# Causal attention as one stream of 32 units, x loaded at its start, and a shared buffer for the last store of each stage

## The reference

```python
# layer 0 attention, per batch b; positions rotate pairs of q and k (RoPE)
q[h] = rope(x @ Wq[h].T)          # 2 heads of 128
k    = rope(x @ Wk.T)             # one key head, shared
v    = x @ Wv.T                   # one value head, shared
p[h] = softmax(q[h] @ k.T / sqrt(128) + causal mask)
out  = concat_h(p[h] @ v) @ Wo.T
y    = layernorm(x + out)
```

## Time and profile before

| what | value |
|---|---|
| median of 3 runs | 2108.05 us (2103.53 to 2110.74) |
| the profiled execution's own time | 2110.27 us |
| its span, first to last instruction | 2108.4 us |
| PE busy | 1884.2 us, 89% of the span |
| DVE, ACT, POOL busy | 75%, 59%, 28% |
| attention | from 0 to about 279.4 us of the span |
| later stages begin at | 283.7, 565.3, 902.8, 1511.6 and 1967.9 us |
| mean granted clock of TensorE | 0.94 of full speed |

### The profile page before, as it was taken

How to read it: one execution, slowest core, us unless ns; L and a number is a source line. 1 busy time by engine, 2 the same in 40 slices (tenths; PEclk the granted TensorE clock), 3 DMA queues, 4 the chain that set the end, 5 groups by cost and what they waited for, 6 DMA issues and landing times. The chain is left out here.

```text
span 2108.4 us, 32001 instructions
## 1 busy us (share of the span) xinstructions
PE 1884.2 (89%) x10615; PEld 1281.7 (61%) x10624; DVE 1571.8 (75%) x3786; ACT 1249.2 (59%) x2554; POOL 597.4 (28%) x767
## 2 busy tenths in 40 slices
PE   7999979999599999669999999999799998995697
PEld 5667644444377777548888887888673444544342
DVE  4554547677447888659999999999533999997498
ACT  3335436656345555168888887887313768876465
POOL 2221216678302222200000000000000777777022
PEclk9999989999699999689999999999768999998799
DMA  2000020000200000000000000000310222222100
GB/s 91 30 30 0 30 88 11 15 6 11 89 22 11 21 11 11 6 20 2 6 16 1 6 16 6 2 7 16 132 62 2 53 59 63 63 68 67 48 26 26
DMA packets 34697, 65.80 MB, mean 31 GB/s; under 512 B 8406, under 2 KB 19743, under 8 KB 33783
## 3 DMA queue, kind: packets, MB, share of 16 engines
q1 hardware_dynamic: 26358, 47.16, 6.6%
q0 software_dynamic: 8192, 16.79, 3.1%
HBM read 51.34 MB, written 12.58 MB: 30 GB/s over the span
## 5 line engine op out<-in xcount | busy, mean ns | idle before, releaser
L2183 DVE SCALAR_TENSOR_TENSOR pk_level<-pk_sums,pk_least 128x1024 f32<-128x1024 f32 x256 | 322.3, 1279 | 22.8 <-ACT pk_sums L2092 21.6
L2092 ACT ACTIVATE pk_sums<-pk_sum 128x512 f32<-128x512 f32 x512 | 278.7, 602 | 94.5 <-PE pk_sum L2302 92.2
L2524 POOL DMA_INDIRECT tk_values<-top_keys_values,tk_index x256 | 241.8, 945 | 197.1 <-DVE tk_index L2744 119.4
L2310 PE MATMUL pk_weights<-product_keys_early_ident,pk_level 128*128 128x128 f32 x2048 | 269.5, 274 | 26.3 <-DVE pk_level L2183 24.3
L2310 PEld LDWEIGHTS pk_weights<-product_keys_early_ident,pk_level 128*128 128x128 f32 x2048 | 226.0, 141 | 52.9 <-DVE pk_level L2183 33.8
L2954 PE MATMUL tk_to_act<-tk_keys,tk_xT 128*128 128x512 f32 x512 | 236.0, 611 | 22.5 <-ACT tk_scores L2611 21.2
L2954 PEld LDWEIGHTS tk_to_act<-tk_keys,tk_xT 128*128 128x128 f32 x512 | 96.2, 195 | 144.2 <-issue 94.7
L1755 PEld LDWEIGHTS er_outs<-experts_early_w,er_hT 128*128 128x128 f32 x1024 | 134.0, 192 | 59.8 <-issue 56.4
L1165 PE MATMUL ml_outs<-experts_early_we,ml_xT 128*128 128x512 f32 x320 | 160.1, 628 | 3.5 <-DVE ml_r L1022 3.5
L2302 PE MATMUL pk_sum<-pk_lay_corners,pk_partsT 96*128 96x256 bf16 x1024 | 154.1, 272 | 0.9 <-ACT pk_sums L2092 0.9
L2742 DVE MAX8 tk_best<-tk_scores 128x8 f32<-128x4096 f32 x32 | 141.2, 4413 | 14.9 <-ACT tk_scores L2611 14.9
(11 more groups left out here) (437 smaller groups left out, 3700.0 us busy)
## 6 DMA issues: line engine op xcount, KB each, us to landing
tk_scores<-top_keys_compress SPq DMA_DIRECT2D x1, 4096.0 KB
tk_values<-top_keys_values,tk_index POOLq DMA_INDIRECT x256, 2.5
att_x_proj<-x_first SPq DMA_DIRECT2D x4, 512.0 KB, 5.3
att_x_res<-x_first SPq DMA_DIRECT2D x4, 512.0 KB, 4.3
x_after_attention<-att_y SPq DMA_DIRECT2D x4, 512.0 KB, 5.0
experts_early_w<-experts_w SPq DMA_DIRECT2D x2, 1024.0 KB
x_after_attention<-ml_y SPq DMA_DIRECT2D x8, 256.0 KB, 2.0
experts_ahead_x<-x_after_attention SPq DMA_DIRECT2D x8, 256.0 KB, 3.4
```

The source lines that it names most:

```text
L2092: act.activation(sums[:, n % SUMS, half * HALF:(half + 1) * HALF], bank[:], ACT.Copy).then_inc(S.free.sem, 1)
L2183: dve.scalar_tensor_tensor(level[:, n % LEVELS, :], sums[:, n % SUMS, :], least[:, t % 2, h:h + 1], sums[:, n % SUMS, :], ALU.is_ge, ALU.m ...
L2310: ins = pe.matmul(weights[:, ch * P:(ch + 1) * P], level[:, n % LEVELS, ch * P:(ch + 1) * P], ident[:], is_transpose=True, start=h == 0 an ...
L2524: pool.indirect_dma_start(out=values[:, slot, k, :], out_offset=None, in_=c["values"], in_offset=bass.IndirectOffsetOnAxis(ap=index[slot][ ...
```

## The change

**Attention becomes one stream.** The loop is gone. 32 units (4 batches of 8) run one behind the other, and the work of a head (now called preparing) is cut in pieces, which PE, ACT, DVE and POOL do between the units of the batch before. The first batch's pieces run before the first unit. In preparing:

- q and k of one tile are a single matmul: xT of the tile stays in the array, 384 columns of weights pass (8 for each batch; swapped weights are no longer needed).
- DVE multiplies the 384 columns with cos, and twice 192 of them, read with a step of 2, with sin. POOL adds 384 columns. PE then transposes three blocks (q of two heads, k) through ring A, and ACT copies them out in two instructions, of 256 and 128 columns.
- Wv and Wo are multiplied with each other once, at the start. v becomes 256 columns wide, so the values' matmul gives the output itself: the copy by DVE and the matmul with Wo are gone. For each block of keys the transposed probabilities of a head stay in the array and 128 columns of v pass: two matmuls of 128 columns instead of one of 256.
- All four batches of x are loaded at the beginning, behind the constants, and kept in SBUF.

**The last store of each stage** but the final one leaves from a buffer (`last`) that belongs to both the stage and the next one. The stage does not wait for its landing; SP waits for it in the next stage (`first_x.stored`), ahead of its loads.

```diff
 class Ahead:
         self.x, self.arrived = room.sb("x", shape), room.sem("arrived")
+        self.last, self.stored = room.sb("last", [P, PER_HALF, P]), room.sem("stored")
...
+        PROJECTED = {1: (0, 1), 2: (2, 3), 3: (4,), 4: (5,), 5: (6,), 6: (7,)}
+        TURNED = {2: (0, 1), 3: (2,), 4: (3, 4), 5: (5,), 6: (6,), 7: (7,)}
+        VALUED = {1: (0,), 2: (1,), 3: (2,), 4: (3,)}
...
+        def in_turn(u):
+            return ([("xT", g) for g in range(HALVES)] if u == 0 else []) + [("qk", t) for t in PROJECTED.get(u, ())] + \
+                   [("v", g) for g in VALUED.get(u, ())] + [("qkT", t) for t in TURNED.get(u, ())]
...
 # SP
+            sp.dma_start(x[:, 0], x_in[0]).then_inc(x_loaded[0], 16)
...
+            for b in range(1, B):
+                sp.dma_start(x[:, b], x_in[b]).then_inc(x_loaded[b], 16)
             next_weights.load(sp)
...
+            sp.wait_ge(y_ready, B * HALVES)
+            sp.dma_start(x_out[B - 1][:, PER_HALF:TILES, :], next_x.last[:]).then_inc(next_x.stored, 16)
+            for i in range(2):
+                sp.wait_ge(stored[i], 16 * (B // 2))
...
 # DVE
+            def turn(b, t):
...
+                dve.tensor_tensor(turned[:, q % 2, 0], both, spread(cos[:, t, :], 1, HEADS + 1), ALU.mult)
+                dve.tensor_tensor(turned[:, q % 2, 1, :, 0::2], both[:, :, 1::2], spread(sin[:, t, 0::2], 1, HEADS + 1), ALU.mult)
+                dve.tensor_tensor(turned[:, q % 2, 1, :, 1::2], both[:, :, 0::2], spread(sin[:, t, 1::2], 1, HEADS + 1),
+                                  ALU.mult).then_inc(V.free.sem, 1)
...
+            for n in range(-UNITS, ALL + 2):
+                if 0 <= n + 1 < ALL:
+                    maxes(n + 1)
+                if 1 <= n <= ALL:
+                    residual(n - 1)
+                if n < ALL and prepared(n):
+                    b, u = prepared(n)
+                    for t in PROJECTED.get(u, ()):
+                        turn(b, t)
+                if n >= 2:
+                    normalise(n - 2)
...
 # PE
+            def project(b, t):
+                pe.wait_ge(A.free.sem, taken_from_A("xT", b, t // PER_HALF))
+                bank = claim_V()
+                pe.matmul(bank[:, 0:COLS], xT[:, t * P:(t + 1) * P], wqk[:], start=True, stop=True).then_inc(V.full.sem, 1)
...
+                        ins = pe.matmul(bank[:, own], probsT[:, n % 2, k, own], v[:, b % 2, k, own],
+                                        start=k == 0 and h == 0, stop=k == u and h == HEADS - 1)
...
+            multiply_weights()
+            for n in range(-UNITS, ALL + 1):
+                if 0 <= n + 1 < ALL:
...
+                    score(n + 1)
+                if n >= 1:
+                    weigh_values(n - 1)
+                if 0 <= n < ALL:
+                    transpose_probs(n)
+                if n < ALL and prepared(n):
...                                   (the pieces of in_turn(u) for the next batch)
...
 # SP of the next stage (here the second one; the third and fourth likewise)
+            sp.wait_ge(first_x.stored, 16)
             load(1)
...
-            sp.wait_ge(stored[1], 16 * B)
+            sp.wait_ge(stored[1], 16 * (B - 1))
```

More of the change, by code:

```diff
@@ new lines, in take_wvo, with take_xT @@
+            def take_wvo():
+                act.wait_ge(wvo_full, 1)
+                act.activation(wvo[:], scores[:, 0, 0:HEADS * P], ACT.Copy).then_inc(wvo_ready, 1)
+            def take_xT(b, g):
+                act.wait_ge(A.full.sem, A.to_take(0))
+                bank = A.take()
+                if b > 0:
+                    act.wait_ge(V.full.sem, made_for_V("qk", b - 1, TILES - 1))
+                act.activation(xT[:, g * HALF:(g + 1) * HALF], bank[:], ACT.Copy).then_inc(A.free.sem, 1)
@@ new lines, in take_probsT @@
+            def take_probsT(n, j):
+                blocks = min(2, n % UNITS + 1 - 2 * j)
+                act.wait_ge(A.full.sem, A.to_take(0))
+                bank = A.take()
+                if j == 0 and n >= 2:
+                    act.wait_ge(V.full.sem, made_for_V("out", n - 2))
+                act.activation(probsT[:, n % 2, 2 * j:2 * j + blocks, :].rearrange("p k n -> p (k n)"),
+                               bank[:, 0:blocks * HEADS * P], ACT.Copy).then_inc(A.free.sem, 1)
+            take_wvo()
@@ new lines, in maxes, with residual @@
+            def maxes(n):
+                keys = (n % UNITS + 1) * P
+                for h in range(HEADS):
+                    dve.wait_ge(scored, n * HEADS + h + 1)
+                    after(dve, exped, (n - KEPT + 1) * HEADS)
+                    dve.tensor_reduce(neg_max[:, n % KEPT, h:h + 1], scores[:, h, 0:keys], AX.X, ALU.max,
+                                      negate=True).then_inc(maxed, 1)
+            def residual(n):
+                b, u = divmod(n, UNITS)
+                s = n % KEPT
+                dve.wait_ge(exped, (n + 1) * HEADS)
+                steps.link(dve.reciprocal(inv_sum[:, s, :], row_sum[:, s, :]))
+                dve.wait_ge(V.full.sem, V.to_take(0))
+                bank = V.take()
+                if u == 0:
+                    dve.wait_ge(x_loaded[b], 16)
+                steps.link(dve.scalar_tensor_tensor(r1[:, n % 2, :], bank[:, 0:P], inv_sum[:, s, 0:1],
+                                                    x[:, b, u, :], ALU.mult, ALU.add))
+                dve.scalar_tensor_tensor(r[:, s, :], bank[:, P:2 * P], inv_sum[:, s, 1:2], r1[:, n % 2, :],
+                                         ALU.mult, ALU.add).then_inc(V.free.sem, 1)
+                dve.wait_ge(V.free.sem, taken_from_V("out", n))
+                norm_stats(steps, dve, r[:, s:s + 1, :], stats[:, s:s + 1, :],
+                           moments[:, s:s + 1, :]).then_inc(moments_ready, 1)
@@ new lines, in normalise @@
+            def normalise(n):
+                b, u = divmod(n, UNITS)
+                s = n % KEPT
+                dve.wait_ge(rstd_ready, n + 1)
+                if u == 0:
+                    after(dve, stored[b % 2], 16 * (b // 2))
+                own = y[:, b % 2, u:u + 1, :]
+                if b == B - 1 and u >= PER_HALF:
+                    own = next_x.last[:, u - PER_HALF:u - PER_HALF + 1, :]
+                last = norm_apply(dve, own, r[:, s:s + 1, :], moments[:, s:s + 1, :], rstd[:, s:s + 1])
+                if u % PER_HALF < PER_HALF - 1:
+                    steps.do(last)
+                else:
+                    steps.settle()
+                    last.then_inc(y_ready, 1)
@@ L2203, in normalise @@
                 after(dve, stored[g % 2], 16 * (g // 2))
[L2204 removed]
+                own = next_x.last if g == GROUPS - 1 else y[:, g % 2]
+                norm_apply(dve, own, r[:], moments[:], rstd[:]).then_inc(y_ready, 1)
             norm_x(0)
```

492 lines of the change are left out of this document (237 added, 255 removed).

## The result

The changed kernel takes **2073.05 us** in the median (4 runs, 2071.28 to 2074.04); the kernel before, on the same chip, 2109.36 (4 runs, 2103.53 to 2110.74). The ratio is 0.9829, 95% interval 0.9813 to 0.9845: 1.7% less time, well clear of the noise, though under 2%. Forecast were 2067 us and a range of 2054 to 2084. One execution of a later kernel, first_batch, took 3148.54 us at a mean granted clock of 0.55 and stands in no median here. The profiled execution took 2072.89 us, with a span of 2070.7 and a mean granted clock of 0.94, as before.

A forecast was written before the change was run, and what follows sets the result against it. The prediction took PE's work and waits to bound attention. From 2110.3 us profiled it took off 32.7 for attention and 8.2 for stage ends, giving 2069.4, or 2067 against the median 2.2 lower; range 2054 to 2084.

The forecast's parts named there:

- What bounds the batch: Attention's stream: PE's order sets the batch, 53.2 us of work plus 4.8 of waits, 58.0 a batch.
- The sum unit by unit: PE's waits in attention, added over small and large units: 3.7 us a batch.
- unseen hand-overs: PE's waits in attention: hand-overs not visible cost more than nothing, so 4.8 us a batch was taken over 3.7.
- The rival with bare loads: Attention's values: 72 more weight loads cost 0.11 each, 7.9 us a batch, 32 in all, total 2099; chance 0.03.
- DVE, ACT, POOL: Attention: their work hides behind PE in the units, DVE at some 34 us and ACT 33 of 58.
- The beginning: Attention's start: DVE's 1.2 us a tile sets the pace, first scores at about 23.8 instead of 26.2, unit 1's at 25.2.
- The sum for attention: All of attention: PE ends at 243.9, last y at 246.7 instead of 279.4, a gain of 32.7 us.
- Stage ends: Five stage ends: barriers come earlier by SP's wait, 2.3, 1.9, 1.7, 0.3 and 2.0, sum 8.2 us, bounds 4 and 10.1.
- The rival by which stage ends give nothing: Stage ends: the next stage starts on something else, or the barrier takes what was won; 2075 us; chance 0.07.
- I count nothing: Pause at attention's end: PE still falls to half clock there, so no gain or loss was taken for the clock.
- The series exchange: Attention: PE waits for each step between engines, 76 us a batch, total 2141, slower than before; chance 0.03.
- The stream that fills nothing: Attention: PE waits as long as before, 8.4 us a batch, total 2079, with head costs 2083; chance 0.13.

The follow-up runs named there:

- first_batch: Changed kernel with only batch 0's pieces reordered, so what unit 0 doesn't need goes behind it; median 2061.41 us, ratio to before 0.9774.
- more_pe: Changed kernel plus two matmuls of 128 columns in each unit, results unused; 2191.79 us, ratio to before 0.9864, on a slower chip.
- ring_order: Changed kernel with only the order of pieces changed, moving transposes of q and k apart from v's fill; 2182.85 us, ratio to before 0.9792, slower chip.
- await_all: Changed kernel with the wait for the last store put back at all five stage ends; 2200.43 us, ratio to before 0.9886, slower chip.
- await_first: Changed kernel with the wait for the last store put back at attention's end only; 2196.12 us, ratio to before 0.9835, slower chip.
- both_orders: Changed kernel with the piece orders of ring_order (batches 1 to 3) and first_batch (batch 0) together; median 2061.22 us, ratio to before 0.9773.
- lump: Changed kernel with all pieces preparing a batch kept together behind unit 6 of the batch before; 2203.91 us, ratio to before 0.9882, slower chip.
- after_third: The changed kernel unaltered, run again as yardstick in the last group on a slower chip; 2191.11 us, ratio to before 0.9829.
- after_again: The changed kernel unaltered, run again on the chip of first_batch and both_orders; median 2071.45 us, ratio to before 0.9821.

## Why the prediction was right, and where it was off

- **What bounds the batch.** Right: PE. 57.8 against 58.0 forecast, and more_pe shows its added work almost whole. The split was off twice, with opposite signs: the values take 16.5 in place of 72 x 0.2225 = 16.0, and the waits are 3.7, not 4.8. That leaves 0.4 of the 57.8, which lie in waits too short for the rows to name and in the transposes: the four instructions of projections at 91.01 take 0.24 more than those at 96.91. The sum unit by unit had given 3.7 as well, and that is in part luck. Its 2.0 for the third bank in units 4 to 7 measured 1.65, its 0.5 for unit 4 0.58 and its 0.3 for unit 7 0.57. But the 0.5 for unit 2 was taken for DVE and is ring A behind ACT's copy of v (0.58), the 0.4 for ring V in unit 1 is at most that 0.24, and the 0.33 in the transposes of x was not in the sum. The 1.1 put on top for unseen hand-overs mostly wasn't there.
- **Weight loads.** 0.227 to 0.230 for a matmul of 128 columns with its own weights, against 0.2225 in the row of v and 0.45 for the 256 columns they replace. The rival with bare loads asked for 0.11 more each (7.9 a batch) and falls; what is left of it is at most 0.5 us a batch. The Trainium skill, "TensorE: Matmul & The Clock Gate", section "The mechanism", says that a weight load overlaps running matmuls only where the row groups differ; these whole-array f32 loads, at 0.227 to 0.230 a matmul, disagree with that sentence. The same section also lets a load run ahead when it goes to the background weight buffer, which the prediction left out; the price agrees with that, but no run here shows which of the two is at work.
- **DVE, ACT, POOL.** Right, and the step of 2 costs nothing that can be seen. From the groups of lines (busy us, mean ns | idle before), two of attention and one of the second stage, which reads PSUM without a step:

```profile
L488 DVE TENSOR_TENSOR att_turned<-att_to_dve,att_cos 128x384 f32<-128x384 f32 x32 | 17.7, 553 | 27.4 <-PE att_to_dve L572 27.4
L489 DVE TENSOR_TENSOR att_turned<-att_to_dve,att_sin 128x192 f32<-128x192 f32 x32 | 11.2, 349 | 0.0
L1086 DVE TENSOR_TENSOR ml_r<-ml_to_dve,experts_ahead_x 128x256 f32<-128x256 f32 x8 | 3.4, 419 | 3.4 <-PE ml_to_dve L1242 3.4
```

0.553 and 0.349 against the forecast 0.56 and 0.36. From 256 to 384 columns without a step it is 0.134 us more, or 0.067 for each 64; 192 columns without a step would by that estimate take 0.419 - 0.067 = 0.352. DVE is at 33 us of a batch (34 forecast), ACT at 31 (33), POOL at 14, as before.

- **The beginning: the step that failed.** "Then DVE's 1.2 us a tile sets the pace" was the sentence. DVE took 1.0 to 1.1 a tile and waited for PE besides; PE's order put all eight projections, the transposes of seven tiles and all of v ahead of the first scores, with waits of 0.45 twice for ACT and 1.28 for POOL. Scores at 26.15 and 27.56 instead of 23.8 and 25.2: 2.4 us. ring_order shows the cause by winning 2.0 of it with the order of the pieces alone, and first_batch shows what a shorter list gives (18.29). A second part had no term in the forecast: the row of projections at 11.15 lasts 2.71 us where the same four instructions at 14.56 last 1.46. PE, idle until 8.42, works there at half speed, though the profile's clock column shows no drop; that is some 1.2 us, in a beginning that before had slow rows too. Of the bound, "no gain" just held (26.15 against 26.18), and "2 us worse" did not (2.4).
- **The sum for attention.** From unit 1's scores to PE's end (243.10 + 3.63 = 246.7) it is 219.2, forecast 218.7. With the 2.4 of the beginning PE ends 2.8 later than the forecast 243.9, and the last y comes 2.9 later: a gain of 29.8 for 32.7.
- **Stage ends.** 8.47 for 8.2, term by term 2.77, 0.14, 1.89, 1.63 and 2.04 for 2.3, 0.3, 1.9, 1.7 and 2.0. The third stage's start does wait for its own x, as its row shows: the load is issued 0.47 behind the last store, as it was issued behind the stores before, so the barrier's gain is taken back. The last stage's start waits for its own x as well, which is why PE won 2.04 there and not the whole wait of 3.0.

```profile
526.96 0.32 SPq L860 DMA_DIRECT2D x_after_attention<-experts_ahead_last  x1
527.43 0.38 SPq L875 DMA_DIRECT2D experts_ahead_x<-x_after_attention  x1
530.66 1.09 PE L214 MATMUL er_to_act<-experts_early_ident,experts_ahead_x 128*128 128x128 f32 x4 [9.36 <-DMA experts_ahead_x<-x_after_attention]
...
1928.08 1.94 PE L214 MATMUL moe_to_act<-experts_early_ident,experts_ahead_x 128*128 128x128 f32 x8 [7.36 <-DMA experts_ahead_x<-x_after_top_keys]
```

  The 0.47 that attention's end gave beyond the forecast is not the wait (1.65, less than the 2.3 I took) but the 1.1 that stay won without it, which I had not priced. The rival by which stage ends give nothing falls with await_all and await_first. That SP's new waits hold up next to nothing also stands: they are 0.5 and 0.4.
- **The clock.** "I count nothing" was right for the pause, but not for the rest: the second stage won 2.2 and the last lost 2.3 through drops that come or go. The same 784 matmul instructions of the second stage keep PE busy for 248.38 us before and 246.20 after, the same 503 of the last for 125.17 and 127.66. That the two cancelled is luck. In first_batch and both_orders such drops didn't cancel, and gave more than the edit.
- **The total.** 2070.7 of span against 2108.4 - 40.9 = 2067.5. The gap of 3.2 is 2.9 from attention, less 0.3 from the pauses, and 0.55 from the lengths of the other stages (-2.19 + 0.14 + 0.29 + 0.01 + 2.3). The other 2.9 up to 6.05 are the step from the profiled execution to the median: I took off 2.2 because that of before lay that much above its median, and that of after lay 0.2 below its own; the rest is what lies around the span and rounding.
- **The rivals.** The series exchange (76 us a batch) is far off; its 0.2 for each hand-over stood on no row. The stream that fills nothing (8.4 of waits) is refuted by the 3.7 of the timeline, and lump shows what it would look like.

## What to carry to other kernels

Software-pipelining a loop's head into the body of the pass before is worth its waits only as far as each piece is apart from what it needs: moving two of them by a place was worth another 3 us over three batches, at the same work on every engine. In the prologue there is no cover at all: follow PE's list in its order, and put only what the first unit needs ahead of it. And when a kernel differs by less than 0.5%, compare it stage by stage with the granted clock beside it before the difference is put down to the edit.

## What the runs showed of the hardware that was not expected

- An f32 matmul of 128 columns with new 128x128 weights costs 0.227 to 0.230 us in a chain of up to 16, half of a 256-column one (0.445 to 0.45) within 3%.
- DVE reading every second f32 of 384 in PSUM takes 0.349 for 192 columns, in line with 0.419 for 256 and 0.553 for 384 that lie together.
- The clock's drops have places in the work: in the second stage all kernels but await_all (1.00) show 0.83 at 50 to 60 us behind its first matmul. Others come or go: the third stage's costs 1.7 us, those of the last stage 2.8.
- On two of the chips the fifth stage took 107 to 135 us longer. Its 256 gathers take POOL 0.94 us each in before and in after_third alike. In after_third ACT waits for 126.1 us in 22 waits at L2714 for something that the profile doesn't name, and in after_again never. No experiment looked for the cause.
